# Attention with talking heads: head mix by four 64x64 blocks a pair, scores by 64x32 blocks, side and distance on GpSimd

## The reference

```python
dots = jnp.einsum('bhid,bhjd->bhij', l2norm(q), l2norm(k)) * 10.0      # 16 heads of 64, 4 memory keys
dots = jnp.einsum('hg,bgij->bhij', W_pre_th, dots)                      # heads mixed ahead of the softmax
dots = jnp.where(causal, mask_value, dots)                              # column j - 4 > row i
dots = jnp.where(dots < top_k(dots, 64)[..., -1:], mask_value, dots)    # 64 largest of a row stay
attn = jnp.einsum('hg,bgij->bhij', W_post_th, softmax(dots))            # heads mixed again
out = ((attn @ v) * head_scale * sigmoid(x @ Wg + bg)) @ Wo
```

## Time and profile before

| | us |
|---|---|
| median of 3 runs (2321.97 to 2326.05) | 2322.53 |
| the profiled execution | 2325.43 |
| its span, first to last instruction | 2323.6 |
| PE busy | 2091.2 |
| DVE busy | 1805.0 |
| ACT busy | 1604.0 |
| POOL busy | 826.4 |

### The profile page before, as it was taken

How to read it: one execution, slowest core, us unless ns; L and a number is a source line. 1 busy time by engine, 2 the same in 40 slices (tenths; PEclk the granted TensorE clock), 3 DMA queues, 4 the chain that set the end, 5 groups by cost and what they waited for, 6 DMA issues and landing times. The chain is left out here.

```text
span 2323.6 us, 55179 instructions
## 1 busy us (share of the span) xinstructions
PE 2091.2 (90%) x16059; PEld 1354.7 (58%) x16060; DVE 1805.0 (78%) x7282; ACT 1604.0 (69%) x4676; POOL 826.4 (36%) x2274
## 2 busy tenths in 40 slices
PE   7995799889988998899889988999899889975997
PEld 3433456666666666666666666666666666663433
DVE  6565489968995899589968995899589958983446
ACT  4442588858885887588758876887688768861543
POOL 3001444345434543444354435442544254311000
PEclk9996799999999999999999999999999999997998
DMA  6002112111211121112111211121012101212002
GB/s 177 0 0 86 24 39 62 43 26 44 61 44 26 43 62 44 26 44 62 44 26 43 62 43 26 44 61 44 26 44 62 43 24 42 65 32 88 1 0 72
DMA packets 113216, 104.69 MB, mean 45 GB/s; under 512 B 34448, under 2 KB 110864, under 8 KB 112912
## 3 DMA queue, kind: packets, MB, share of 16 engines
q1 hardware_dynamic: 108000, 96.65, 16.4%
q10 hardware_dynamic: 4912, 4.46, 0.6%
HBM read 19.14 MB, written 12.71 MB: 14 GB/s over the span
## 5 line engine op out<-in xcount | busy, mean ns | idle before, releaser
L1052 PE MATMUL bankC<-R,E 128*128 128x128 f32 x2560 | 350.0, 286 | 44.5 <-POOL R L1403 44.4
L1052 PEld LDWEIGHTS bankC<-R,E 128*128 128x128 f32 x2560 | 336.4, 201 | 83.9 <-POOL R L1403 50.0
L1036 PE MATMUL bankB<-raw,mixpre 128*128 128x76 f32 (+37 forms) x1024 | 355.2, 434 | 19.2 <-DMA raw<-SC 18.8
L1252 ACT ACTIVATE S<-bankB,aim_first 128x68 f32<-128x68 f32 (+56 forms) x456 | 231.4, 511 | 119.2 <-PE bankB L1036 118.8
L1403 POOL TENSOR_SCALAR R<-mixpost,rinv 128x128 f32<-128x128 f32 x512 | 185.4, 375 | 297.8 <-DVE rinv L1562 297.6
L1498 DVE TENSOR_SCALAR_CACHE_REDUCE S<-S,minus_thr 128x68 f32<-128x68 f32 (+56 forms) x456 | 217.8, 514 | 94.3 <-POOL minus_thr L1396 93.3
L1387 POOL TENSOR_TENSOR S<-S,diagmask 128x8 f32<-128x8 f32 x512 | 111.4, 222 | 488.8 <-ACT S L1252 434.9
L1558 DVE SCALAR_TENSOR_TENSOR E<-S,limit,E 128x68 f32<-128x68 f32 (+56 forms) x456 | 234.8, 550 | 36.3 <-ACT E L1278 6.8
L1025 PE MATMUL bankD<-KT,QT 64*64 64x132 f32 (+8 forms) x2304 | 191.1, 406 | 59.9 <-ACT qk L1187 30.9
L1278 ACT ACTIVATE E<-S,nmax 128x12 f32<-128x12 f32 (+56 forms) x512 | 241.1, 533 | 0.0
L1078 PEld LDWEIGHTS bankM<-PT,V 128*64 128x64 f32 x5120 | 177.7, 137 | 101.0 <-issue 90.3
(11 more groups left out here) (177 smaller groups left out, 3975.0 us busy)
## 6 DMA issues: line engine op xcount, KB each, us to landing
X_first<-in_L_attn_x_dram ACTq DMA_DIRECT2D x8, 512.0 KB, 9.9
x<-X_first SPq DMA_DIRECT2D x8, 512.0 KB, 2.9
xt<-x SPq DMA_DIRECT2D x32, 128.0 KB, 2.3
x<-xt SPq DMA_DIRECT2D x32, 128.0 KB, 2.5
X_last<-x SPq DMA_DIRECT2D x8, 512.0 KB, 6.6
out_dram<-X_last SPq DMA_DIRECT2D x8, 512.0 KB, 2.8
raw<-SC SPq DMA_DIRECT2D x8, 258.0 KB, 3.0
raw<-SC SPq DMA_DIRECT2D x8, 254.0 KB, 2.9
```

What stands on the lines that cost most here:

```text
L1036: last = nc.tensor.matmul(bankB[n % 2][:, 0:wide(n)], W.mixpre[:, :], raw[n % RAWS][:, 0:wide(n)], start=True, stop=True)
L1052: last = nc.tensor.matmul(bankC[n % 2][:, jb * P:(jb + 1) * P], E[n % EBUFS][:, jb * P:(jb + 1) * P], R[n % RBUFS][:, :], start=True, stop ...
L1252: nc.scalar.activation(S[n % SBUFS][:, 0:wide(n)], src, ACT.Identity, bias=W.aim_first[:, group(n)]).then_inc(S_out, 1)
```

## The change

1. *Head mix.* `mixpre` becomes 128x64: for the upper and for the lower 64 partitions a 64x64 matrix of 16 heads by 4 queries. The rows of a transfer now hold 4 queries of group `n0` and 4 of group `n0 + 1`, so that `mix_pair(n0)` needs both transfers; it makes both groups with four 64x64 matmuls, of the four quadrants of the array. It stands where `mix(n0)` stood, and waits for the eviction of `n0 - 1`; ScalarE evicts both groups there. In odd groups the two halves of the queries are crossed, so `mixpost` and `diagmask` have a second version. A transfer of an even group is 8 columns wider.
2. *Scores.* Queries are laid out so that the transfer can take these rows: `qT` copies with two copies a half, and each 64x64 score matmul becomes two of 64x32 (64 rows of the contraction, 32 of the output).
3. *Side and distance.* `side` and `order` are made on GpSimd, one pair behind `threshold` and ahead of `scaled_mix` (`sides`): `side` is doubled and `order` is its square, compared with squares in `iotaM`. VectorE keeps `flip`.

```diff
         link(ts(wpre[:, :], wpre[:, :], QK_SCALE, None, ALU.mult))
 
-        pre = W.mixpre[:, :].rearrange("p (c i k) -> p c k i", c=2, i=IG)
+        pre = W.mixpre[:, :].rearrange("p (c i k) -> p c k i", c=2, i=QUARTER)
         for h in range(H):
-            ts(pre[:, h // IG, h % IG, :], own[:, :], wpre[:, h:h + 1], None, ALU.mult)
-            last = ts(W.mixpost[:, h * IG:(h + 1) * IG], own[:, :], wpost[:, h:h + 1], None, ALU.mult)
+            ts(pre[:, h // IG, h % IG, :], own4[:, :], wpre[:, h:h + 1], None, ALU.mult)
+            for odd, mine in enumerate((own, crossed)):
...
                     sp.wait_ge(mixed, n - RAWS + 1)
-                w = group_width(n)
+                w = group_width(n // 2 * 2 + 1)
                 sp.dma_start(raw[n % RAWS][:, 0:w], SC[g:P:IG, :, 0:w]).then_inc(raw_in[n % RAWS], 16)
...
-                            for side_ in range(2):
+                            for c, side_ in ((0, 0), (0, 1), (1, 0), (1, 1)):
                                 for r in range(2):
-                                    rows, cols = slice(64 * r, 64 * r + 64), slice(64 * side_, 64 * side_ + 64)
-                                    pair = 4 * side_ + quarter
-                                    last = nc.tensor.matmul(bankD[cols, r, i * s[3]:(i + 1) * s[3]],
-                                                            QT[rows, pair, HALF * hh:HALF * hh + HALF],
-                                                            KT[rows, pair, first:first + s[3]],
+                                    rows, at = slice(64 * r, 64 * r + 64), 64 * c + 32 * side_
+                                    pair, lo = 4 * side_ + quarter, HALF * hh + 32 * c
+                                    last = nc.tensor.matmul(bankD[at:at + 32, r, i * s[3]:(i + 1) * s[3]],
+                                                            QT[rows, pair, lo:lo + 32], KT[rows, pair, first:first + s[3]],
                                                             start=True, stop=True, skip_group_check=True)
                         return last
                     pe_use(pe, s, emit)
 
-            def mix(n):
-                pe.wait_ge(raw_in[n % RAWS], 16 * (n // RAWS + 1))
-                if n >= 2:
-                    pe.wait_ge(S_out, n - 1)
-                last = nc.tensor.matmul(bankB[n % 2][:, 0:wide(n)], W.mixpre[:, :], raw[n % RAWS][:, 0:wide(n)],
-                                        start=True, stop=True)
-                if is_wide(n):
-                    if n // GPT >= 2:
-                        pe.wait_ge(x_added, n // GPT - 1)
-                    last = nc.tensor.matmul(bankT[:, P:P + MEM], W.mixpre[:, :], raw[n % RAWS][:, 512:J],
-                                            start=True, stop=True)
-                last.then_inc(mixed, 1)
+            def mix_pair(n0):
+                for n in (n0, n0 + 1):
+                    pe.wait_ge(raw_in[n % RAWS], 16 * (n // RAWS + 1))
+                if n0:
+                    pe.wait_ge(S_out, n0)
+                parts = [(r, cols, slice(HALF * r, HALF * r + HALF), raw[(n0 + (r + cols) % 2) % RAWS])
+                         for cols in range(2) for r in range(2)]
+                if is_wide(n0 + 1):
+                    if n0 // GPT >= 2:
+                        pe.wait_ge(x_added, n0 // GPT - 1)
+                    for r, cols, rows, src in parts:
+                        if r:
+                            nc.tensor.matmul(bankT[HALF * cols:HALF * cols + HALF, P:P + MEM], W.mixpre[rows, :],
+                                             src[rows, 512:J], start=True, stop=True, skip_group_check=True)
+                for r, cols, rows, src in parts:
+                    w = wide(n0 + r)
+                    last = nc.tensor.matmul(bankB[r][HALF * cols:HALF * cols + HALF, 0:w], W.mixpre[rows, :],
...
                 if live:
-                    mix(n0)
...
-                    mix(n0 + 1)
...
             def qT(j):
                 for half in range(2):
-                    act_use(act, ("qT", j, half), lambda: nc.scalar.copy(
-                        QT[:, 4 * half:4 * half + 4, :].rearrange("p q (u i g) -> p (q u) i g", u=2, i=IG),
-                        bankD[:, half, :].rearrange("p (q g i) -> p q i g", q=8, i=IG)))
+                    def emit():
+                        dst = QT[:, 4 * half:4 * half + 4, :].rearrange("p q (u c i g e) -> p c (q u) e i g", u=2, c=2,
+                                                                        i=QUARTER, e=2)
+                        src = bankD[:, half, :].rearrange("p (q g c e i) -> p c q e i g", q=8, c=2, e=2, i=QUARTER)
+                        for c in range(2):
+                            last = nc.scalar.copy(dst[:, c, :, :, :, :], src[:, c, :, :, :, :])
+                        return last
+                    act_use(act, ("qT", j, half), emit)
...
                 if live:
                     evict(n0)
+                    evict(n0 + 1)
...
-                    evict(n0 + 1)
...
+            def sides(ns):
+                cols = ring(ns)
+                pool.wait_ge(signs_done, ranked_upto(ns[-1]))
+                nc.gpsimd.tensor_tensor(side[:, cols], signs[:, cols], W.middle[:, in_batch(ns)],
+                                        ALU.add).then_inc(side_done, len(ns))
+                pool.wait_ge(side_done, ranked_upto(ns[-1]))
+                nc.gpsimd.tensor_tensor(order[:, cols], side[:, cols], side[:, cols],
+                                        ALU.mult).then_inc(order_done, len(ns))
+
             def scaled_mix(n):
...
                     threshold(ranked_in(n0))
+                if ranked_in(n0 - 2):
+                    sides(ranked_in(n0 - 2))
...
                     cols = ring(ranked)
-                    dve.wait_ge(signs_done, ranked_upto(ranked[-1]))
-                    nc.vector.scalar_tensor_tensor(
-                        out=side[:, cols], in0=signs[:, cols], scalar=0.5, in1=W.middle[:, in_batch(ranked)],
-                        op0=ALU.mult, op1=ALU.add).then_inc(side_done, len(ranked))
                     dve.wait_ge(side_done, ranked_upto(ranked[-1]))
-                    bits = side[:, cols].bitcast(I32)
-                    flipped = step(nc.vector.tensor_scalar(flip[:, cols], bits, 31, 0x7FFFFFFF, ALU.arith_shift_right,
-                                                           ALU.bitwise_or))
-                    ordered = step(nc.vector.tensor_scalar(order[:, cols].bitcast(I32), bits, 0x7FFFFFFF, None,
-                                                           ALU.bitwise_and))
+                    flipped = step(nc.vector.tensor_scalar(flip[:, cols], side[:, cols].bitcast(I32), 31, 0x7FFFFFFF,
+                                                           ALU.arith_shift_right, ALU.bitwise_or))
                     dve.wait_ge(tk, flipped)
...
                 if ranked:
+                    dve.wait_ge(order_done, ranked_upto(ranked[-1]))
                     for n in ranked:
-                        dve.wait_ge(tk, max(at[n], ordered))
+                        dve.wait_ge(tk, at[n])
                         nc.vector.scalar_tensor_tensor(
                             out=picked[n % 2][:, :], in0=W.iotaM[:, :], scalar=order[:, col(n)], in1=top[n % 2][:, :],
                             op0=ALU.is_equal, op1=ALU.mult,
```

43 lines of the change are left out of this document (29 added, 14 removed).

## The result

The changed kernel takes 2309.72 us (median of 4 runs, 2307.09 to 2313.22), the kernel before, run beside it, 2324.29 (2321.97 to 2326.08). The ratio is 0.9948, with a 95% interval of 0.9923 to 0.9972: 12 us faster (7 to 18), where I forecast 41 less. The profiled execution took 2313.22 us.

A forecast was written before the change was run, and what follows sets the result against it. VectorE bounds the wide stretch, mostly TensorE the narrow one. Per batch 3.6 + 0.4 + 2.4 - 0.5 - 0.6 = 5.3 us, eight gain 42, less 1 for setup: forecast 2281 us, range 2244 to 2314.

The forecast's parts named there:

- VectorE's part: Side and distance leave VectorE: 0.19 us a pair, 19 wide pairs, 3.6 us a batch, plus 0.4; cost on GpSimd 0.
- narrow mixes: Shorter mixes of 24 groups in the narrow stretch (1149 to 1237 us): 2.4 us of TensorE a batch gained.
- setup: Before the batches: some 25 more small VectorE instructions beside a busy TensorE, costing 1 us in all.
- Transfers and ScalarE: A pair needs both transfers: 0.6 us more waiting for `raw` in the narrow stretch; score copy not later.
- rival B: TensorE's clock falls once more a batch after standing still, 1.8 us each, 15 in all: 2296; chance 0.07.
- rival D: Two new GpSimd operations a pair hold VectorE through its memory port, 0.4 us a pair: 18 slower, 2342; chance 0.09.
- Head mix: Four 64x64 blocks run as one, so a pair of mixes costs one width; only the narrow stretch's 2.4 us a batch shows.
- the main doubt: Most wrong if the narrow stretch is not TensorE's, for then 1.3 us a batch are missing.
- Rival A: In the narrow stretch ScalarE's copies and GpSimd take TensorE's place; only VectorE's gain remains: 31 less, 2291; chance 0.14.
- Scores: Eight 64x32 tiles run at once, 0.92 us as before; extra passes cost 0.04 us a quarter, 0.5 us a batch.
- rivals C and E: C: scores take two rounds, 2312, chance 0.13. E: eight new passes don't hide, 0.14 us a quarter, 2291, chance 0.05.

The follow-up runs named there:

- side_only: Kernel before with only side and distance moved to GpSimd; head mix, scores and ScalarE's order as before: 2308.32 us, ratio 0.9927.
- scores_32: Kernel before with side and distance on GpSimd, plus each 64x64 score block split into two of 64x32: 2306.03 us, ratio 0.9939.
- fixed_twice: both_fixed with each narrow pair's mix (first 26 groups of a batch) done twice, same result: 2307.79 us, ratio 0.9933.
- both_fixed: Changed kernel with both edits: second eviction back behind the score copy, second transfer of a half tile's start on ScalarE's queue: 2291.0 us, ratio 0.9858.
- mix_only: Changed kernel with side and distance back on VectorE; head mix, scores and ScalarE's order stay changed: 2349.87 us, ratio 1.0119.
- evict_split: Changed kernel with the second eviction of a pair back behind ScalarE's score copy, values and qT: 2309.51 us, ratio 0.9947.
- two_queues: Changed kernel with the second transfer of each half tile's first pair issued by ScalarE behind its last score copy: 2303.74 us, ratio 0.9928.
- filled: Changed kernel plus eight idle 512-column score passes once a batch, where TensorE stands at the 25th pair: 2308.23 us, ratio 0.9939.
- fixed_filled: both_fixed plus the eight idle passes once a batch at the 25th pair: 2296.16 us, ratio 0.9883.

## Why the prediction was wrong, step by step

The runs give each term of the sum a measurement, each beside one partner kernel:

```
term                          forecast   measured   by
VectorE's part                   -32       -17      side_only
scores in eight tiles             +4        +3      scores_32 against side_only (+-5)
narrow mixes                     -19       -17      fixed_twice against both_fixed (+17)
transfer, evictions               +5       +21      both_fixed against the changed kernel
setup                             +1        ?
sum                              -41       -12      (the measured terms: -10)
```

That the measured terms add up is in part the choice of partners. VectorE's part is worth 17 us in the kernel before, 25 in the one with both edits (against 2315.44) and 40 in the changed kernel (against 2349.87).

**Transfers and ScalarE** is the step that failed most, by 16 us: "ScalarE's evictions both come while scores run, so the score copy is not later". At 1105 us the copy stands behind the second eviction (1105.19 to 1105.80 by the row of two from 1104.67 on), and TensorE's waits for `SC` ahead of scores grew from 26.4 to 45.1 us. That sum is no measure of the loss, though: it is 43.3 with the eviction put back, and 49.4 with both edits, in a kernel that is 21 us faster. I looked at when the evictions start and not at what is queued behind them. The transfer's 0.6 us, once a batch, was short as well: in the narrow stretch of that batch TensorE's wait for `raw` is 3.2 us where it was 1.8. The two together cost 21 us; apart they show 0 and 5. That either alone leaves TensorE standing somewhere long enough for its clock would explain this, but it isn't shown: the count below is 15 and 16 with the one or the other, 18 with neither and 11 with both.

**The clock (rival B, 0.07)** names a mechanism that the runs show at three places, but not its forecast of one more fall a batch: by the count below there are 18 falls after the change and 16 before, at other places, and the mean granted clock is 0.948 against 0.957. I priced a fall at 1.8 us; it costs VectorE's cycle 1.0 (cycle 26 before: 8.0 in four of eight batches, 8.6 to 9.0 in the others) to 1.7 (cycle 0 with both edits: 8.09 without it, 9.78 in the same batches where the passes bring it on), 1.8 in cycle 6 with both edits (4.20 and 6.0), and 3.0 in the batch of the rows above. I had the reason too, "A TensorE with less to do stands still more often", and left it out of the sum. The count of places where 8 or 16 passes behind a wait take longer than at full clock, in one trace each (seven batches, the first left out, for the first two places, eight for the third):

```
kernel         start of batch  cycle 6    turn in cycle 24  sum of 22   less than before, us
               (3.7 us)        (3.6-3.9)  (1.95-2.05)
before              7              5            4              16            0
side_only           6              3            3              12           17
scores_32           7              1            2              10           14
mix_only            6              7            7              20          -28
changed kernel      3              7            8              18           12
evict_split         6              7            2              15           12
two_queues          1              7            8              16           17
filled              5              7            0              12           14
both_fixed          2              3            6              11           33
fixed_filled        7              5            0              12           27
```

The count doesn't order the times: twelve falls go with 14, 17 and 27 us less. How much of the 12, or of the 21, us is the clock's stays open.

**VectorE's part** missed by 15 us. 0.16 us a pair is there in most wide cycles where I had 0.19: 19 x 0.03 x 8 = 5 us. Cycles 15, 26 and 27 of side_only are 0.66, 0.43 and 0.32 us longer than before instead of shorter: with 0.19 for each, 2.0 us a batch, 16 in all. "`R` is then some 0.2 us later ... Cost 0" was wrong at one place: `side` waits there for its count, `R` starts 2.0 us behind `rinv` (0.7 of them pass before the threshold's own count is there, so only a part is `side`'s), and GpSimd's multiplication behind it holds the product with `E` (2.22 us for 0.49), where before it held `picked` for 1.03. That is rival D's lock, by an old long operation and not by the new short ones; the product's mean is 556 ns now and 550 before, long collisions included. These 21 us are more than the 15 that are missing; traces of single executions don't settle the difference. `flip` never waits for `side` in the changed kernel, and it does where `side` stands behind `R`: there the step's reasoning held.

**Head mix.** Right: four blocks run as one, 0.79 us for a pair, and the narrow time was worth 17 of 19 us once the two costs were gone, and 11 while they were there (each within 7, so the two are not told apart for certain). What I called the main doubt, that the narrow stretch might not be TensorE's, was unfounded in the kernel with both edits. Rival A (TensorE's part is given back) describes the result, and ScalarE's copies had a part in it as it says; but they didn't take TensorE's place for good, since the order of one eviction and the queue of one transfer bring 21 us back.

**Scores.** Right; rivals C and E are out. Twice the passes take the same 0.99 us. The 64 small passes take 0.71 us at full clock where 32 took 0.65: 2 ns for each pass added. The Trainium skill's fixed cost of about 60 cycles a matmul (TensorEngine Tiling (Array Packing), Instruction Overhead), an estimate of 0.2 us a quarter by that page, doesn't show here.

**Additivity.** The sum took the two parts as separate. They are not: 17 less and 28 more make 12 less, and repaired, 17 and 8 less make 33. That one shared wait, and the clock behind it, is counted in both is a guess that no run shows. Why four batches keep the clock in cycle 6 with both edits, and none does in the changed kernel, stays open.

## What to carry to other kernels

When one engine's instructions are brought forward in its queue, list what is queued behind them and who waits for that, even where the moved ones seem to run in time. Where TensorE gets less work but the same waits, look at each wait and at the row behind it: price the passes at the lower clock there, as part of the sum and not as a rival. Don't take a longer sum of waits for the size of a loss; here it stayed while 21 us went. Test repairs together as well as apart; here two that showed 0 and 5 us gave 21.

## What the runs showed of the hardware

Giving TensorE 1.1 us of useless passes while it stood 1.8 us made 16 passes behind them take 2.05 us instead of 3.2 to 3.8, in eight batches of eight. Standing 2.21 us left the clock at 1.00 and a projection at 3.67 us; standing 3.42 us gave 0.51 and 6.69 us for the same eight passes. The length of that stand isn't the whole of it: 2.36 us at the same place left 3.67 (changed kernel), and 1.89 gave 6.42 (both edits, another batch). And a two-input GpSimd operation of 1.9 us held one VectorE instruction until about its own end, three times (2.22 us for 0.49, 1.72 for 0.22, and 1.03 for 0.22 before the change), but not the two `max` that ran beside it before the change in 0.78 us, as usual. The Trainium skill (SBUF — State Buffer, Terms) describes an exclusive lock between the two engines for a whole instruction; the trace agrees for the three held instructions, which read two tensors each. `max` reads one, and the entry doesn't say which instructions ask for the lock, so it isn't a case against it.
